# Gate and routing moved inside the edge sort, and layer statistics inside the return, in a two-layer graph kernel

## The reference, cut to what matters

```python
# layer 0, mixture of 8 experts on the normalised rows
logits = x @ gate_w + gate_b
probs = softmax(logits); idx = argmax(probs); prb = probs[idx]
pos = (cumsum(one_hot(idx)) * one_hot).sum(-1) - 1
kept = pos < C
buf[idx, pos] = x
hmid = relu(buf @ w1 + b1); ybuf = hmid @ w2 + b2
y = nan_to_num(ybuf[idx, min(pos, C - 1)] * (prb * kept))
# layer 1, factor of each edge (53125 edges, 10 inputs)
h = silu(edge_len_emb @ fc_w1 / sqrt(10)) * SILU_NORM
msg_rad = h @ fc_w2 / sqrt(64)
# layer 1, expert gate: softmax and sums over edges grouped by target
denom = segment_sum(exp(e - max), dst)  # 32768 edges and a loop per node
```

## Time and profile before

| | us |
|---|---|
| median of 3 runs | 3196.61 (3190.63 to 3198.87) |
| profiled execution | 3201.74 |
| its span | 3200.0 |
| busy PE / DVE / POOL / ACT | 2347.8 / 2022.9 / 1772.2 / 1366.0 |
| sort, from DVE's first copy to its last cast | 1080.27 to 1263.85 |
| experts' first scatter | 1396.39 |
| return's first instruction | 1654.30 |

### The profile page before, as it was taken

How to read it: one execution, slowest core, us unless ns; L and a number is a source line. 1 busy time by engine, 2 the same in 40 slices (tenths; PEclk the granted TensorE clock), 3 DMA queues, 4 the chain that set the end, 5 groups by cost and what they waited for, 6 DMA issues and landing times. The chain is left out here.

```text
span 3200.0 us, 41075 instructions
## 1 busy us (share of the span) xinstructions
PE 2347.8 (73%) x11127; PEld 1534.7 (48%) x11128; DVE 2022.9 (63%) x4085; ACT 1366.0 (43%) x3768; POOL 1772.2 (55%) x1789
## 2 busy tenths in 40 slices
PE   0798677777777366689988777777777788888781
PEld 0454455555554255336642423233335677777760
DVE  3444799999998887200036289999995542222588
ACT  0122556556553133332115388888883122222230
POOL 1244788878773045537763277777771147777200
PEclk9899888888887655589987889999989779999895
DMA  5000666666661000234412133333330121111004
GB/s 121 20 33 30 211 202 203 203 210 201 205 205 39 4 2 2 87 88 123 123 46 58 50 101 99 101 98 101 100 100 7 27 68 36 36 36 36 16 1 172
DMA packets 163816, 287.79 MB, mean 90 GB/s; under 512 B 55320, under 2 KB 99357, under 8 KB 163598
## 3 DMA queue, kind: packets, MB, share of 16 engines
q0 software_dynamic: 79568, 187.15, 21.6%
q1 hardware_dynamic: 68628, 75.89, 7.7%
q10 hardware_dynamic: 15402, 22.14, 2.0%
HBM read 248.79 MB, written 36.25 MB: 89 GB/s over the span
## 5 line engine op out<-in xcount | busy, mean ns | idle before, releaser
L2298 PE MATMUL cv_ps<-cv_msg,cv_hot 128*128 128x512 f32 x880 | 438.9, 657 | 164.5 <-DVE acc L2348 114.0
L2285 POOL DMA_INDIRECT cv_x<-x_tab,e_src x440 | 448.2, 1019 | 195.4 <-issue 97.5
L926 POOL DMA_INDIRECT at_kv<-kv_tab,e_src x440 | 470.3, 1069 | 147.3 <-issue 93.9
L1982 POOL DMA_INDIRECT pairs<-gating_pair,gating_place x288 | 279.1, 969 | 234.5 <-DVE gating_place L1947 93.1
L2719 POOL DMA_INDIRECT gs_h<-h_tab,fc_q x312 | 296.8, 951 | 178.6 <-issue 92.6
L2298 PEld LDWEIGHTS cv_ps<-cv_msg,cv_hot 128*128 128x128 f32 x880 | 180.7, 211 | 422.4 <-ACT cv_msg L2311 207.5
L2311 ACT ACTIVATE cv_msg<-cv_x,factors 128x64 f32<-128x64 f32 x1320 | 356.6, 333 | 0.0
L2348 DVE TENSOR_TENSOR acc<-acc,cv_ps 128x256 f32 x880 | 307.9, 414 | 41.8 <-PE cv_ps L2298 35.3
L2309 ACT ACTIVATE cv_msg<-cv_x,factors 128x256 f32<-128x256 f32 x440 | 217.8, 495 | 128.2 <-DMA cv_x<-x_tab,e_src 128.2
L1062 PE MATMUL at_a<-at_kv,at_hot_e 128*128 128x264 f32 x880 | 250.7, 414 | 7.1 <-DVE at_kv L1135 5.0
L1037 PE MATMUL at_q<-q_parts,at_hot_n 128*128 x1320 | 216.4, 317 | 40.8 <-DVE at_kv L1119 32.1
(11 more groups left out here) (538 smaller groups left out, 4620.7 us busy)
## 6 DMA issues: line engine op xcount, KB each, us to landing
x_w<-in_L_ffn_w SPq DMA_DIRECT2D x16, 1024.0 KB, 7.9
at_rel_row<-e_rel_rows SPq DMA_DIRECT2D x55, 256.0 KB, 4.8
experts_out<-gs_y ACTq DMA_DIRECT2D x20, 512.0 KB, 2.6
x_y<-experts_out SPq DMA_DIRECT2D x20, 512.0 KB, 4.7
at_kv<-kv_tab,e_src POOLq DMA_INDIRECT x440, 3.9
cv_x<-x_tab,e_src POOLq DMA_INDIRECT x440, 2.8
kv_tab<-p_qkv SPq DMA_DIRECT2D x25, 256.0 KB, 2.0
gs_h<-h_tab,fc_q POOLq DMA_INDIRECT x312, 2.4
```

The lines of the kernel that those rows point to most:

```text
L926: nc.gpsimd.indirect_dma_start(out=kv[:, t % (RING * Q4), 0:2 * D], out_offset=None, in_=kv_tab, in_offset=bass.IndirectOffsetOnAxis(ap=e. ...
L1982: nc.gpsimd.indirect_dma_start(out=pairs, out_offset=bass.IndirectOffsetOnAxis(ap=place_i[:, c:c + 1], axis=0), in_=pair[:, c, :], in_offs ...
L2285: nc.gpsimd.indirect_dma_start(out=xg[:, i % RT, u, :], out_offset=None, in_=x_tab, in_offset=bass.IndirectOffsetOnAxis(ap=e.src[:, t:t + ...
L2298: nc.tensor.matmul(ps[u % R][:, :], hot[:, i % 2, u, :], msg[:, i % 2, u, :], start=True, stop=True).then_inc(summed, 1)
```

## The change

- The gate's work moves into the counting loop: in turn `i` ACT normalises block `i`, PE transposes it and scores block `i - 2`, ACT (not DVE) copies the transposes, DVE adds the bias of block `i - 3`.
- The routing chain runs on DVE between the counting loop and the bases of the rank loop. The whole `XN` is gone: ACT makes one normalised row block per turn of the rank loop into a ring of four (`sent_rows`), and GpSimd sends it, one send and one scatter per turn.
- The radial net's buffers (`ef.h`, `ef.rad_space`, `ef.emb_space`) are made first and lie under the sort's tables, which are dead by the time they are needed; its weights and first two loads come during the rank loop.
- A stage `radial0` replaces gate and routing: 10 loads of the net (`FIRST`) and 48 scatters. Scatters are now split 48 / 48 / 192 over sort, radial stage and experts, before 80 / 32 / 176. The return has 16 loads instead of 13.
- Row statistics are taken group by group in the return; `layer_stats` is gone.

```diff
-def layer_stats(nc, k, name):
-
-    with Scope(nc) as s:
-        stats = LayerStats(nc, s, k, name)
-        with nc.Block() as block:
-            @block.vector
-            def _(dve):
-                for b in range(NB):
-                    stats.block(b)
-                stats.end(dve)
-        stats.finish()
...
-def gate0(nc, k, XN, logits, pairs, pair, place_i):
...
-def route0(nc, k, XN, logits, buf, slot_i, factor, ef):
...
+def radial0(nc, k, ef, pairs, pair, place_i):
...
+                ef.load(sp, 2, ef.FIRST)
...
+                ef.activate(act, ps_h, ps_r, 0, ef.FIRST)
...
+                ef.multiply(pe, ps_h, ps_r, 0, ef.FIRST)
...
+                total = ef.R * ef.FIRST
+                scatter.run(nc, k, pool, pairs, pair, place_i,
+                            pace=lambda n: [(ef.hid, n * total // (scatter.turns * U))] if n * total >= scatter.turns * U else [])
...
-        scatter = Scatter(s, "x0_sc_", GATE_SCATTER, C2 // U)
+        scatter = Scatter(s, "x0_sc_", RADIAL_SCATTER, C2 // U)
...
-                ef.load(sp, ef.HALF, ef.LOADS)
+                ef.load(sp, ef.FIRST, ef.LOADS)
...
+                    for b in range(g * B5, (g + 1) * B5):
+                        stats.block(b)
+                stats.end(dve)
+
+
+SORT_SCATTER = 6
+RADIAL_SCATTER = SORT_SCATTER + 6
+
+
+def sort_and_route(nc, k, edge_index, pairs, pair, place_i, buf, slot_i, factor, ef):
...
-        work = s.sb("so_work", [P, 4 * U * P], BF)
+        work = ef.h[:, :, :].rearrange("p a q -> p (a q)").bitcast(BF)
+        assert 2 * ef.h.shape[1] * ef.h.shape[2] == 4 * U * P
+        early = [x[:, :, :].rearrange("p a q -> p (a q)").bitcast(BF).rearrange("p (i u d) -> p i u d", u=U, d=P)
+                 for x in (ef.rad_space, ef.emb_space)]
+        LENT = early[0].shape[1]
         lo_t = work[:, 0:2 * U * P].rearrange("p (h u d) -> p h u d", h=2, u=U)
         same = work[:, 2 * U * P:4 * U * P].rearrange("p (h u d) -> p h u d", h=2, u=U)
...
+        later = s.sb("so_lo", [P, C2 // U - 2 * LENT, U, P], BF)
+
+        def lo(i):
+            return early[i // LENT][:, i % LENT] if i < 2 * LENT else later[:, i - 2 * LENT]
...
+        XR = 4
+        sent_rows = s.sb("r0_rows", [P, XR, D])
...
+                sp.wait_ge(zeroed, 1)
+                sp.dma_start(buf[0:SLOTS, :].rearrange("s d -> (s d)").rearrange("(p m r) -> p m r", p=P, r=run),
+                             wide(sent_rows[:, 0:2, :].rearrange("p x d -> p (x d)")[:, 0:run].unsqueeze(1),
+                                  [P, per_part // run, run])).then_inc(emptied, 16)
                 sp.wait_ge(iotas, 2)
                 sp.dma_start(pairs[0:1, :], edge[0:1, 0, 0, :]).then_inc(ended, 16)
                 sp.dma_start(pairs[C2 * P + 1:(C2 + 1) * P, :].rearrange("(a r) b -> a r b", a=1), edge[:, 1, 0:P - 1, :]).then_inc(ended, 16)
                 sp.wait_ge(ended, 32)
+                sp.wait_ge(emptied, 16)
+                ef.weights(sp)
+                sp.wait_ge(turned, 4 * LENT)
+                ef.load(sp, 0, 2)
...
-                scatter.run(nc, k, pool, pairs, pair, place_i, placed)
+                pool.wait_ge(routed, 1)
+                pool.wait_ge(emptied, 16)
+                columns = scatter.turns * U
+
+                def upto_turn(i):
+                    return i if i <= NB else NB + (i - NB) * (columns - NB) // (turns - NB)
+                for i in range(turns):
+                    if i < NB:
+                        n = P if i < NB - 1 else LAST
+                        pool.wait_ge(ready, i + 1)
+                        nc.gpsimd.indirect_dma_start(
+                            out=buf, out_offset=bass.IndirectOffsetOnAxis(ap=send_i[0:n, i:i + 1], axis=0),
+                            in_=sent_rows[0:n, i % XR, :], in_offset=None).then_inc(gone[i % XR], 16)
+                    for c in range(upto_turn(i), upto_turn(i + 1)):
+                        if c >= 2 * U and c % U == 0:
+                            pool.wait_ge(scatter.sent[c // U % 2], 16 * U * (c // U // 2))
+                        pool.wait_ge(placed, max(c // U + 1, i))
+                        scatter.one(nc, pairs, pair, place_i, c // U, c)
...
+                def turn_block(b):
+                    pe.wait_ge(normed, b + 1)
+                    if b >= 2:
+                        pe.wait_ge(kept_x, b - 1)
+                    for x in range(KC):
+                        ins = nc.tensor.transpose(ps_t[b % 2][:, x, :], xn[:, b % 2, x * P:(x + 1) * P], k.ident[:, :])
+                    ins.then_inc(turned_x, 1)
+
+                def score_block(b):
+                    pe.wait_ge(kept_x, b + 1)
+                    if b >= 2:
+                        pe.wait_ge(taken, b - 1)
+                    for x in range(KC):
+                        ins = nc.tensor.matmul(ps_g[b % 2][:, 0:NE], xT[:, b % 2, x, :], k.gate[:, x, :], start=(x == 0), stop=(x == KC - 1))
+                    ins.then_inc(done, 1)
...
+                    if i < NB:
+                        turn_block(i)
+                    if 2 <= i < NB + 2:
+                        score_block(i - 2)
+                pe.wait_ge(chosen, 1)
+                rhs = rt[:, 3].rearrange("p b e -> p (b e)")
+                nc.tensor.matmul(ps_in, k.upper[:, :], rhs, start=True, stop=True)
+                nc.tensor.matmul(ps_all, k.ones[:, :], rhs, start=True, stop=True).then_inc(ranked, 1)
...
+                    if i < NB:
+                        if i >= 2:
+                            act.wait_ge(turned_x, i - 1)
+                        normed_block(nc, k, act, i, xn[:, i % 2, :], normed)
+                    if 1 <= i <= NB:
+                        act.wait_ge(turned_x, i)
+                        if i >= 3:
+                            act.wait_ge(done, i - 2)
+                        nc.scalar.activation(xT[:, (i - 1) % 2], ps_t[(i - 1) % 2][:, 0:KC, :], ACT.Copy).then_inc(kept_x, 1)
                     act.wait_ge(counted, i + 1)
                     nc.scalar.activation(upto[:, i * U:(i + 1) * U, :].rearrange("p u n -> p (u n)"), ps_c[i % 2], ACT.Copy).then_inc(kept, 1)
+                act.wait_ge(asked, 1)
+                nc.scalar.activation(rt[:, 1], rt[:, 0], ACT.Exp).then_inc(exped, 1)
+
+                def row(b):
+                    if b >= NB:
+                        return
+                    if b >= XR:
+                        act.wait_ge(gone[b % XR], 16 * (b // XR))
+                    normed_block(nc, k, act, b, sent_rows[:, b % XR, :], ready)
+                act.wait_ge(emptied, 16)
+                act.wait_ge(ended, 32)
+                row(0)
+                row(1)
 
                 def lower(i):
                     h = i % 2
...
                     lower(i)
                     if i + 1 < turns:
                         round_start(i + 1)
+                    row(i + 2)
...
+                    if 3 <= i < NB + 3:
+                        dve.wait_ge(done, i - 2)
+                        v.tensor_tensor(logits[:, i - 3, :], ps_g[(i - 3) % 2][:, 0:NE], bias[:, :], ALU.add).then_inc(taken, 1)
                 c.link(v.tensor_tensor(not_before[:, :], wide(k.count_col[:, 0:1], [P, P]), k.count_row[:, 0:P], ALU.is_ge))
                 c.link(v.tensor_scalar(not_before[:, :], not_before[:, :], -1.0, None, ALU.mult))
+                dve.wait_ge(taken, NB)
+                c.link(v.tensor_reduce(rr[:, 0], logits[:, :, :], AX.X, ALU.max))
+                v.tensor_tensor(rt[:, 0], logits[:, :, :], wide(rr[:, 0].unsqueeze(2), S), ALU.subtract).then_inc(asked, 1)
+                dve.wait_ge(exped, 1)
...
+                dve.wait_ge(ranked, 1)
+                whole = ps_all.rearrange("p (b e) -> p b e", e=NE)
...
+                v.tensor_copy(send_i[:, :], rr[:, 9]).then_inc(routed, 1)
+                dve.wait_ge(routed, 1)
...
-    HALF = LOADS // 2
+    FIRST = 10
...
-                    sort_edges(nc, k, a["L1_ffn_edge_index"], pairs2, pair, place_i)
-                    XN = t.sb("XN", [P, NB, D])
-                    logits = t.sb("logits", [P, NB, NE])
                     slot_i = t.sb("slot_i", [P, NB], I32)
                     factor = t.sb("factor", [P, NB])
-                    gate0(nc, k, XN, logits, pairs2, pair, place_i)
                     ef = EdgeRadial(nc, t, a, a["attr"], a["emb_t"], e1, 128.0 ** -0.5 * 16.0 ** -0.5)
-                    route0(nc, k, XN, logits, slots, slot_i, factor, ef)
+                    sort_and_route(nc, k, a["L1_ffn_edge_index"], pairs2, pair, place_i, slots, slot_i, factor, ef)
+                    radial0(nc, k, ef, pairs2, pair, place_i)
                     experts0(nc, k, a, slots, slots_out, pairs2, pair, place_i)
-                    return0(nc, k, slots_out, slot_i, factor, ef, angular)
+                    stats = LayerStats(nc, t, k, "n2_")
+                    return0(nc, k, slots_out, slot_i, factor, ef, angular, stats)
+                    stats.finish()
...
-                layer_stats(nc, k, "n2_")
```

237 lines of the change are left out of this document (73 added, 164 removed).

## The result

| | before | after |
|---|---|---|
| median of 5 runs, us | 3196.61 (3190.63 to 3201.82) | 3174.70 (3171.06 to 3179.93) |
| profiled execution, us | 3201.74 | 3171.06 |

What follows compares the result with a forecast made beforehand. No engine is busy over 73% of the span, so stages were summed: sort +23.6, gate and routing -57.4, experts +7.6, return +2.3 = -23.9 us. Against the median 3196.61 that gives 3172.7 us, own range 3165 to 3184, chance 0.60.

Steps and rivals of the forecast that it cites:

- Counting loop: In the sort: 25 turns grow from 1.14 to 1.62 us through TensorE's added gate work, +12.0 us (+4.3 to +21).
- Routing chain: In the sort, ahead of the tables' bases: about thirty small dependent VectorE operations now stand there, +10.3 us (8 to 13).
- Rank loop: In the sort: ScalarE's row per turn is covered by TensorE's wait for VectorE, turns stay about 3.4 us, 0 us.
- Rival 2: Rank loop: ScalarE becomes the late engine, 25 x 0.5 = +12.5 us, total 3185 us; chance 0.13.
- Tail and gap: Sort's end: three scatters behind the last but one cast, +1.3 us; the 8.85 us wait before the radial stage stays.
- Radial stage: Replaces 122.5 us of gate and routing; GpSimd's 48 scatters end it after 60.7 us, 65.1 with 4.4 behind: -57.4 us.
- Experts: 192 scatters instead of 176, GpSimd becomes the last engine: 265.5 us against 257.9, +7.6 us (0 to +9).
- Return: Return and statistics: three more loads at full clock +11.1 us, statistics stage and entry gone -8.8, net +2.3 us.
- rival 1: TensorE reaches 2.4 GHz sooner: counting loop -7.7 us, return -10.5 us, total 3155 us; chance 0.14.
- VectorE as the lighter side: Return: VectorE busy 21.26 of 29 us in the second half, so 25 statistics (8.26 us) fit in at no cost.
- Rival 3: Return: the clock stays at half, 11 of 16 loads each cost 3.5 us more, +38 us, total 3211 us; chance 0.08.
- the prediction's own signs: Expected in the trace: counting-loop weight loads near full, no GpSimd wait over 1 us after the first expert, return ending with ScalarE's store.

Runs made afterwards that it cites:

- Experiment 4: Changed kernel with the counting loop's bias add one turn later (block i - 4 in turn i): the loop took 49.9 us instead of 55.4.
- experiment 10: Changed kernel with ScalarE making each normalised row of the rank loop twice: the loop took 128.0 us, against 126.5 to 128.5 with one row.
- experiments 9: Changed kernel with the bias add one turn later, scatters split 64 / 32 / 192 and spread evenly, 9 loads in the radial stage: 3590.1 us, ratio to before 0.9883.
- experiment 8: Changed kernel with the bias add one turn later and scatters split 48 / 32 / 192 / 16, the last in the return: 3570.6 us, ratio to before 0.9843.
- experiment 7: Changed kernel, two variants: 16 scatters in the radial stage and 224 in the experts (13.8 us behind them); a 10.8 us pause ending the radial stage (4.65 us left).
- experiment 2: Changed kernel with 13 loads of the net in the radial stage and 13 in the return, instead of 10 and 16: 3596.6 us, ratio to before 0.9872.
- experiment 5: Changed kernel again, unedited, twice on slower chips: 3601.7 and 3584.4 us against 3626.5 for the kernel before, ratios 0.9905 and 0.9899.
- experiment 1: Kernel before with only the row statistics moved group by group into the return: 3635.1 against 3632.5 us, ratio 1.0005.

## Why the prediction was right, point by point

*Counting loop, +12.0 said, +8.4 measured.* The step that failed is TensorE's price: 1.21 us of the gate plus 0.37 for counting, added up to 1.58 a turn. Experiment 4 shows 1.39, 1.17 for the gate and 0.22 for the counts. The 0.37 was the busy time of eight matmuls that stood alone; with others behind them the next one starts 0.22 us after the first. So a pair of turns was 2.97 us and not 3.24. That TensorE and the crossing set the turn was right; with an add that comes one turn later 5.5 of the 8.4 us go.

*Routing chain, +10.3 said.* From 1140.75 to 1151.38, 10.6 us, with 1.30 of it a wait for the Exp. In the sort it counts 9.7, since waits of VectorE's before and behind it became about 1 us shorter in all.

*Rank loop, 0 said.* Turns of 3.45 us in both kernels, 118.3 against 117.5 us as a whole; experiment 10 shows room beyond that. Rival 2 is out.

*Tail and gap.* The three scatters stood behind the last cast but one, as said. The wait in front of the radial stage went from 8.85 to 8.61 us.

*Radial stage, -57.4 said, -55.8 measured.* Scatters end it, 60.7 us from first to last, as said. Behind them it took 6.2 us to GpSimd's next, not 4.4.

*Experts, +7.6 said, +13.9 measured.* Their scatters took 261.9 us (261.1 said), and after the first expert GpSimd waits for a mark once, 1.68 us at 1521.8. TensorE ends 14.8 us ahead of the last scatter's end. The failed step is the 4.4 us for landing and change of stage, taken from a stage of 32 scatters. Here it is 9.9. GpSimd's wait was 4.94 and 4.98 us behind 32 scatters (experiments 9 and 8), 6.24 behind 48 in three traces (6.4 to 7.1 in four others, in three of which ScalarE's last store ended the stage), 8.61 behind 73 issues, 9.62 behind 89, 8.6 to 11.1 behind 192 and 13.8 behind 224. On the slower chips the last output stores fall into the wait behind 192, so not all of it need be GpSimd's; in the profiled pair the last store had been issued 22 us before the stage's end. The 8.85 us behind the old sort's 80 and, again, behind the old experts' 176 stood in the earlier trace rows; reading them beside the gate's 4.4 would have shown that it isn't a constant. The rest behind the landing starts only when GpSimd's part ends (experiment 7). Why 192 cost no more than some 90 is not settled: from 32 to 89 a step is about 0.08 us.

*Return, +2.3 said, -8.0 measured.* The step that failed is the clock. The sum kept the 43 us at 0.50 of the earlier trace rows; in the profiled execution it rose after 13. That is the return's half of rival 1; its other half, the counting loop at full clock, did not come. The price of the loads held: 11.1 us for three, as experiment 2 shows. The last store moves by half a microsecond with each microsecond of the rise (67.6 us after a rise at 13, 74.8 at 28, 78.4 at 35). With the rise at 43 it would have gone at about 82 and the next gather come at about 88, 2.5 us later than before: an estimate, and nearly the forecast.

A second step, VectorE as the lighter side, fails once the clock rises early. With the statistics VectorE needs 9.2 + 5 x 12.7 = 72.7 us and is a floor: with the statistics inside, twelve traces end their last one at 72.2 to 73.0 us. It took back 4 of the 14 us by which the early rise moved the last store.

The early rise is no effect of the change: experiment 5 has both an early and a late one in one kernel, and experiment 1 an early one with the loads of the kernel before. With an early rise in both kernels the return would end at about the same time (77 by experiment 1's estimate, 77.7 measured). So the -8.0 us are the clock of two executions and not the change's. At equal clocks the table's sum would be -19 to -21 us instead of -29.7, an estimate. That the medians differ by only 21.9 would fit with rises that vary from run to run; the unprofiled runs don't show it.

*Rival 3* names the right thing to fear. With the rise at 35 us the return is 7 us longer, not 38; no trace held half clock throughout.

*The signs.* Three of the prediction's own signs failed beside the return's clock: TensorE's weight loads filled 38.63 of 55 us in the counting loop and not nearly all, GpSimd had its one wait above 1 us in the experts, and the return ended with VectorE and not with ScalarE's store.

The total came out right by luck in part, since missed terms cancel: +6.3 us in the experts and +1.6 in the radial stage against -10.3 in the return and -3.4 in the sort. In the profiled pair they leave -5.8 us.

## What to carry to other kernels

Where one engine issues many indirect transfers, count a stage's issues twice: 1.27 us each while they run, and a wait behind the last that grows with their number (here 5 us after 32, 14 after 224). When work is moved into a stage, add up each engine's whole list there, since a lighter engine becomes the floor (VectorE's 72.7 us) and then neither a load saved nor a faster clock counts beyond it. Before a stage of two kernels is compared, look at when the granted clock rose in each: here that alone made up the difference of the return. Let a consumer that sits in a producer's loop lag one turn more than the data needs: it lets the slower engine catch up in the other's long operations, and gave back two thirds of this loop's loss.

## What the runs showed of the hardware

- The time at which TensorE's clock rises to 2.4 GHz differs between executions of one kernel: 13 and 35 us after the return's start, with TensorE busy for 33.7 and 33.6 of the first 36 us. Over all traces of the return it is 12 to 43 us. Between 13 and 35 it is worth 11 us to the last store (67.5 against 78.4).
- Eight short matmuls that take 0.37 us by themselves cost TensorE 0.22 us of a turn when others stand behind them, at half clock.
- From the end of GpSimd's last indirect transfer to the next stage it took 5 us after 32 of them and 13.8 after 224, and behind 48 and a pause of 10.8 us there were still 4.65 us.
- Beside VectorE's large operations 14 of 16 scatters took 1.15 to 1.58 us instead of 0.97 (experiment 8).
- The same kernel takes 13 to 14% longer on other chips, and there the rank loop is longer with more issues of GpSimd's (73: 127 us, 80 in the old sort: 142, 89: 154), while on the first chip it does not (73 and 80: 3.45 us a turn). What the engines wait for in those pauses isn't in the trace.
